# A graph kernel's edge sort: the block-number comparison of a row is written with two tables instead of one and a scalar

## The chip, the cores and the metric

The kernel runs on one core of a Trainium2 chip. The metric is the device time of one execution in microseconds (us), as the median of several runs. A core has a matmul engine (PE, with its weight loads shown apart as PEld), a vector engine (DVE), an activation engine (ACT), GpSimd (POOL) and a queue engine that issues transfers (SP). They run their own instruction streams and meet only at semaphores.

## The reference

A graph of 6,250 nodes with 64 features and 200,000 edges goes through four layers, each added to its input and normalised over the features. What matters here is that every layer gathers rows of the source nodes and sums them at the destination nodes:

```python
edge_index = jnp.stack([src, dst])
x = _layernorm(x + _L0_gnn_ref(x, edge_attr_8, edge_attr_16, edge_weight, ..., src, dst), axis=-1)
x = _layernorm(x + _L1_gnn_ref(x, edge_index, edge_weight), axis=-1)
x = _layernorm(x + _L2_gnn_ref(x, edge_index, L2_gnn_W1, L2_gnn_b1, L2_gnn_W2, L2_gnn_b2), axis=-1)
x = _layernorm(x + _L3_gnn_ref(x, edge_index, L3_gnn_W1, L3_gnn_b1, L3_gnn_W2, L3_gnn_b2), axis=-1)
```

Layer 0 also computes, for each edge, `silu(edge_feats @ W1 + b1) @ W2 + b2` for two sets of attributes. Those two small networks are evaluated while the edges are sorted.

## The kernel before

Nodes are split into 50 blocks of 125 by their number modulo 50. `prepare` works out each edge's block numbers and writes a row of sort keys (`key_rows`) and a row of destination block numbers (`block_rows`, bf16) to memory. `sort_edges`, the function that the change touches, then moves each edge into the bucket of its pair (destination block, source block): a memory row of 70 numbers goes to a slot that is the bucket's start plus the edge's rank in it. Later stages (`build_graph`, `smooth`, `polynomial`, `convolve`) work on the sorted rows. A barrier of all engines stands between the sort and `build_graph`.

The sort runs over 200 groups of 8 tiles of 125 edges (1,000 edges), with two sets of buffers `u` used in turn. For each group:

- SP loads `key_row`, `block_row` and `attrs`, once DVE has released the rows (`rows_read`) and PE has read the attributes (`hidden_ps`).
- DVE, in `group_hots`, copies the group's table (L345) and makes three one-hot tables by comparison: `hot_d` and `hot_s` (125 x 400, L352 and L353) from a table of block numbers and a column of each edge, and `hot_dt` (50 x 1000, L354), which has the block number in the partition and the edge along the row. The semaphore `hots` is raised by L354.
- PE waits for `hots`, and for each of the 8 tiles multiplies the running `count` with `hot_dt` (`ps_r`, L300), adds the tile's own counts (`ps_c`, L304), and lets ACT copy the new count (L272). Between them it does the two halves of the hidden layer (`ps_h`, L293) and the output layer (`ps_m`, L314), and after the second tile two small products for the group before (`ps_f`, L321 and L323), which need DVE's `spills` (L383, semaphore `flagged`).
- DVE, in `places`, which it runs for the group before the one whose one-hot tables it has just made, computes the rank of each edge (`same`, L373, eight times; `picked`, L379; `base`, L381), forms the output rows (L387 to L390), waits for `ps_f` (L392) and ends with the slot numbers `row_at` (L401).
- POOL issues 8 indirect transfers per group (L243), which read `row_at` and write the rows to their slots.

On DVE the order is written out by hand: one-hot tables of a group, then the places of the group before, with nothing in parallel. The column `lane_col` holds each partition's own number in float32.

Of the kernel before, what the change touches and what calls it, by code (L numbers as in the profile page):

```python
# [10 lines left out]
NB = 50  # L11
NL = N_NODES // NB
TE = 125
NT = N_EDGES // TE
G = 8
# [120 lines left out]
def sort_edges(nc, io, tbl, key_rows, block_rows, sorted_rows, zeros, zeroed, n_spilled):  # L136

    with ExitStack() as ctx:
# [13 lines left out]
        block_row = [sb(f"block_row{u}", [NB, G * TE], BF16) for u in two]  # L152
# [4 lines left out]
        hot_dt = [sb(f"hot_dt{u}", [NB, G * TE], BF16) for u in two]  # L157
# [19 lines left out]
        lane_col = sb("lane_col", [TE, 1], F32)  # L177
# [16 lines left out]
        with nc.Block() as blk:  # L194
# [139 lines left out]
            def _(dve):  # L334
# [5 lines left out]
                def group_hots(g, it, u, first):  # L340
                    g_is_0 = isinstance(g, int) and g == 0
                    dve.wait_ge(loaded[u], 64 * it + 64)
                    if not first:
                        dve.wait_ge(mixed, g - 1)
                    dve.tensor_copy(grp[u][:, :, 0:8], tbl[:, bass.ds(g * G, G), :]).then_inc(step, 1)  # L345
                    dve.wait_ge(step, 1 if g_is_0 else STEPS * g - (STEPS - 2))
                    dve.scalar_tensor_tensor(grp[u][:, :, 8], grp[u][:, :, 6], float(NB), grp[u][:, :, 7],
                                             ALU.mult, ALU.add)
                    dve.scalar_tensor_tensor(grp[u][:, :, 9], grp[u][:, :, 6], float(NB * CAP), grp[u][:, :, 7],
                                             ALU.mult, ALU.add)  # L350
                    iota3 = iota_blocks[:].unsqueeze(1).to_broadcast([TE, G, NB])
                    dve.tensor_tensor(hot_d[u][:], iota3, grp[u][:, :, 6:7].to_broadcast([TE, G, NB]), ALU.is_equal)  # L352
                    dve.tensor_tensor(hot_s[u][:], iota3, grp[u][:, :, 7:8].to_broadcast([TE, G, NB]), ALU.is_equal)  # L353
                    dve.tensor_scalar(hot_dt[u][:], block_row[u][:], lane_col[0:NB, 0:1], None,  # L354
                                      ALU.is_equal).then_inc(hots, 1)

                def link(ins, value):
# [6 lines left out]
                def places(g, it, u, done):  # L364
# [37 lines left out]
                    assert k[0] == STEPS - 1  # L402

                group_hots(0, 0, 0, True)
                group_hots(1, 0, 1, True)
                places(0, 0, 0, 1)
                with dve.Fori(1, NG // 2) as it:
                    group_hots(2 * it, it, 0, False)
                    places(2 * it - 1, it - 1, 1, 1)
                    group_hots(2 * it + 1, it, 1, False)  # L410
                    places(2 * it, it, 0, 1)
# [1550 lines left out]
```

## Time and profile before

| | us |
|---|---|
| median of 3 runs | 8770.59 |
| lowest and highest run | 8768.96, 8785.42 |
| profiled execution, its own time | 8773.64 |
| span of that execution | 8771.9 |
| PE busy over the span | 6998.2 |
| DVE busy over the span | 5907.1 |
| ACT busy over the span | 4550.5 |
| POOL busy over the span | 2836.6 |
| first and last transfer of the sorted rows starts at | 448.33, 2910.12 |

The busy times are those of the span of 8771.9 us; 1.7 us of the execution lie outside it. The last row tells where the sort lies in the span: about 28% of it. The span's 40 equal slices are 219 us each, so the sort fills slices 3 to 14.

### The profile page before, as it was taken

To read this page: it belongs to the slowest core of one execution; us is meant where nothing else is said; L and a number is where in the kernel's file an instruction comes from. 1 tells how busy PE (TensorE), PEld (TensorE's weight loads), DVE (VectorE), ACT (ScalarE), POOL (GpSimd) and SP (SyncE) were. 2 spreads that over 40 slices of the span, in tenths; PEclk is the share of its full clock that TensorE was granted. 3 is DMA by queue.
4 is the path that set the end of the run, shared out by engine and by line. 5 is a ranking of instruction groups with operands and counts; after the bars stand their busy time and mean duration, and the time that the engine had idled before them with its cause. 6 is when DMAs were issued, how large, how long until landed. Compare 5 with 4: busy or idle time off the path is not lost. (4 is left out here: it accounts for less than half of the span.)

```text
span 8771.9 us, 281023 instructions
## 1 busy us (share of the span) xinstructions
PE 6998.2 (80%) x98174; PEld 5919.3 (67%) x98174; DVE 5907.1 (67%) x15840; ACT 4550.5 (52%) x14713; POOL 2836.6 (32%) x2937
## 2 busy tenths in 40 slices
PE   0399999999999789889883886887876878876876
PEld 0155555555555788888873786776875878875766
DVE  1277766666777788888875886886785655555555
ACT  0222222222222688888873997997983444443443
POOL 0078888888888544444440000000000000000000
PEclk9999999999999999999996998998998989887978
DMA  9222222322222466666664887887874545542534
GB/s 385 82 58 60 60 59 60 60 60 60 59 59 60 151 205 208 204 204 208 202 191 149 286 288 245 286 285 246 290 252 139 178 157 166 172 157 95 173 127 135
DMA packets 781209, 1430.10 MB, mean 163 GB/s; under 512 B 294298, under 2 KB 361580, under 8 KB 776696
## 3 DMA queue, kind: packets, MB, share of 16 engines
q1 hardware_dynamic: 571720, 967.63, 35.6%
q10 hardware_dynamic: 116928, 381.29, 12.6%
q0 software_dynamic: 92048, 74.42, 4.3%
q8 instruction: 312, 5.11, 0.2%
q14 instruction: 201, 1.65, 0.1%
HBM read 987.87 MB, written 433.30 MB: 162 GB/s over the span
## 5 line engine op out<-in xcount | busy, mean ns | idle before, releaser
L243 POOL DMA_INDIRECT sorted_rows<-sort_rows,sort_row_at x1600 | 1975.6, 1235 | 519.1 <-issue 506.0
L1452 ACT ACTIVATE smooth_msg<-smooth_ps_l,smooth_w_rows 128x64 f32<-128x64 f32 x7500 | 1591.3, 404 | 224.2 <-PE smooth_ps_l L1516 210.2
L272 ACT ACTIVATE sort_count<-sort_ps_c 50x50 bf16<-50x50 f32 x1600 | 331.2, 207 | 1984.0 <-PE sort_ps_c L304 1983.9
L1210 PE MATMUL poly_ps<-parts,poly_cast 125*128 125x192 bf16 x12500 | 1089.5, 252 | 203.4 <-DVEq L1289 106.3
L1210 PEld LDWEIGHTS poly_ps<-parts,poly_cast 125*128 125x128 bf16 x12500 | 1073.6, 101 | 219.0 <-issue 135.4
L1176 ACT ACTIVATE poly_cast<-poly_mat 128x1280 bf16<-128x1280 uint8 x500 | 609.2, 1262 | 771.1 <-PE poly_ps L1210 550.5
L1516 PE MATMUL smooth_ps_l<-parts,smooth_src 125*128 125x64 bf16 x22500 | 800.3, 195 | 261.3 <-DMA smooth_src<-src_rows 151.6
L1516 PEld LDWEIGHTS smooth_ps_l<-parts,smooth_src 125*128 125x128 bf16 x22500 | 720.1, 99 | 302.4 <-ACT smooth_msg L1452 130.1
L314 PE MATMUL sort_ps_m<-sort_w,sort_hidden 128*125 128x64 f32 x3200 | 879.3, 430 | 0.0
L1530 PE MATMUL smooth_ps_s<-smooth_msg,smooth_hot 128*128 128x64 bf16 x7500 | 763.5, 194 | 133.3 <-DVE smooth_last_part L1664 106.3
L300 PEld LDWEIGHTS sort_ps_r<-sort_count,sort_hot_dt 50*125 50x125 bf16 x1600 | 283.2, 177 | 835.8 <-issue 583.3
L1661 DVE TENSOR_TENSOR smooth_rest<-smooth_msg 128x640 f32<-128x640 f32 x750 | 617.7, 824 | 305.9 <-ACT smooth_msg L1452 265.2
L293 PE MATMUL sort_ps_h<-sort_attrs,sort_w 24*128 24x500 f32 x800 | 811.6, 1115 | 2.5 <-DMA sort_attrs<-in_attr_t 2.5
L1530 PEld LDWEIGHTS smooth_ps_s<-smooth_msg,smooth_hot 128*128 128x128 bf16 x7500 | 684.7, 98 | 164.3 <-issue 116.2
L701 ACT ACTIVATE graph_hot_t<-graph_ps_t 128x1024 bf16<-128x1024 bf16 x625 | 641.8, 1027 | 289.4 <-PE graph_ps_t L744 267.6
L1530 PE MATMUL smooth_ps_s<-smooth_rest,smooth_hot 128*128 128x64 bf16 x7500 | 761.1, 194 | 3.1 <-issue 3.1
L1530 PE MATMUL smooth_ps_s<-smooth_last_part,smooth_hot 128*128 128x64 bf16 x7500 | 759.7, 193 | 4.1 <-issue 4.1
L314 PEld LDWEIGHTS sort_ps_m<-sort_w,sort_hidden 128*125 128x125 f32 x3200 | 732.1, 320 | 41.2
L777 PE MATMUL graph_ps_kv<-kv_parts,graph_hot_t 125*128 125x128 bf16 x7500 | 694.4, 221 | 0.0
L1530 PEld LDWEIGHTS smooth_ps_s<-smooth_last_part,smooth_hot 128*128 128x128 bf16 x7500 | 683.6, 99 | 4.2 <-issue 4.2
L1530 PEld LDWEIGHTS smooth_ps_s<-smooth_rest,smooth_hot 128*128 128x128 bf16 x7500 | 685.1, 98 | 1.1 <-issue 1.1
L671 POOL TENSOR_TENSOR graph_parts<-graph_parts 128x260 f32<-128x260 f32 x625 | 388.5, 622 | 912.5 <-DVE graph_hot L828 909.9
(313 smaller groups left out, 14892.5 us busy)
## 6 DMA issues: line engine op xcount, KB each, us to landing
smooth_src<-src_rows SPq DMA_DIRECT2D x750, 320.0 KB, 4.3
smooth_hot<-hot_rows SPq DMA_DIRECT2D x750, 320.0 KB, 4.7
poly_mat<-counts_t ACTq DMA_DIRECT2D x504, 400.0 KB, 3.6
sorted_rows<-zeros ACTq DMA_DIRECT2D x100, 875.0 KB, 13.4
graph_edges<-sorted_rows SPq DMA_DIRECT2D x125, 700.0 KB
conv_mat<-counts ACTq DMA_DIRECT2D x208, 400.0 KB, 3.6
hot_rows<-graph_hot SPq DMA_DIRECT2D x125, 640.0 KB, 3.6
src_rows<-graph_hot_t SPq DMA_DIRECT2D x125, 640.0 KB, 3.5
```

The costliest lines, as they stand in the source:

```text
L243: pool.indirect_dma_start(out=sorted_rows, out_offset=bass.IndirectOffsetOnAxis(row_at[u][:, j:j + 1], 0), in_=rows[u][:, j, :], in_offset ...
L293: nc.tensor.matmul(ps_h[h][:, 0:H * TE], w1[:], attrs[u][:, h * H * TE:(h + 1) * H * TE], start=True, stop=True).then_inc(hidden_ps, 1)
L314: last = nc.tensor.matmul(ps_m[u][0:TE, t * D:(t + 1) * D], hidden[u][:, t * TE:(t + 1) * TE], w2[:], start=True, stop=True, skip_group_ch ...
L671: pool.tensor_tensor(p[:, :, GROUP:2 * GROUP], p[:, :, 0:GROUP], high(p, 0), ALU.subtract)\
L701: act.activation(hot_t[x.b][:, :, :, x.s, :].rearrange("p e t v d -> p e t (v d)"), ps_t[x.g % 2][:].rearrange("p e t v d -> p e t (v d)") ...
L777: last = nc.tensor.matmul(ps_kv[u][:, 2 * t + v], s_t, kv_parts[:, s, i], start=i == 0, stop=i == 2, skip_group_check=True)
L1176: act.activation(cast[u][h][:, DVE_S:HR, :], mat[u][h][:, DVE_S:HR, :], ACT.Copy)\
L1210: last = nc.tensor.matmul(ps[u][:, 0:3 * D], cast[u][h][0:NL, s, :], parts[:, b].rearrange("p i d -> p (i d)"), start=b == 0, stop=b == NB ...
L1452: last = act.activation(at[:, s, :], ps_l[g % 2][h][:, i * D:(i + 1) * D], ACT.Copy, scale=w_rows[:, u, c * CHUNK + s:c * CHUNK + s + 1])
L1516: last = nc.tensor.matmul(ps_l[g % 2][h][:, i * D:(i + 1) * D], src[c][0:NL, b, :], parts[k % 2][:, c * CHUNK + b, j, :], start=j == 0, st ...
L1530: last = nc.tensor.matmul(ps_s[u][:, 0:D], hot[c][:, i // 2, :, i % 2], part[:, i, :], start=c == 0 and i == 0 and j == 0, stop=c == N_CHU ...
L1661: dve.tensor_tensor(rest[c][:], msg[c][:], high(msg[c]), ALU.subtract).then_inc(firsts, 1)
```

## The change

One instruction of `group_hots` is written in another form, with the same result. In the old form each element of `block_row` is compared with one number that its partition holds, given as a scalar operand. In the new form it is compared, element by element, with a second table operand, and that table is the same column read again for each of the 1,000 elements.

```diff
@@ group_hots @@
-                    dve.tensor_scalar(hot_dt[u][:], block_row[u][:], lane_col[0:NB, 0:1], None,
+                    dve.tensor_tensor(hot_dt[u][:], block_row[u][:], lane_col[0:NB, 0:1].to_broadcast([NB, G * TE]),
                                       ALU.is_equal).then_inc(hots, 1)
```

Every engine has the same number of instructions in the same order as before, with the same waits. `hot_dt` and `block_row` are bf16 and `lane_col` is float32 in both forms.

## Rows read from the trace of the kernel before

**Rows 1.** The page: PE's busy share and granted clock, tenths, in 40 slices.
```profile
PE   0399999999999789889883886887876878876876
...
PEclk9999999999999999999996998998998989887978
```
**Rows 2.** Busy us, 1600 to 2200: PE, PEld, DVE, ACT, POOL, then granted clock.
```profile
1600.00:2200.00 600.00, 570.99 (x1856) 356.06 (x1856) 409.03 (x1851) 138.86 (x490) 480.94 (x391) 1.00 0.28 59
```
**Rows 3.** PE in order of time: start, length; the same step in three groups.
```profile
430.17 0.30 PE L300 MATMUL sort_ps_r<-sort_count,sort_hot_dt 50*125 50x50 bf16 x1
...
442.48 0.30 PE L300 MATMUL sort_ps_r<-sort_count,sort_hot_dt 50*125 50x50 bf16 x1
...
2879.85 0.30 PE L300 MATMUL sort_ps_r<-sort_count,sort_hot_dt 50*125 50x50 bf16 x1
```
**Rows 4.** Who waited for whom, 400 to 2700 us: total, times, longest (us).
```profile
DVE sort_spill_ps L392 <- PE sort_ps_f L323: 465.0, 184, 2.9
...
PE sort_ps_r L300 <- ACT sort_count L272: 109.8, 371, 0.3
...
PEld sort_ps_r L300 <- DVE sort_hot_dt L354: 1.5, 1, 1.5
```
**Rows 5.** Instructions on the tile of L354: count, shortest/median/longest in ns.
```profile
L354 DVE TENSOR_SCALAR sort_hot_dt<-sort_block_row,sort_lane_col x200: 464/481/905, 429.6 to 2873.6; 50x1000 bf16<-50x1000 bf16 x100
```
**Rows 6.** DVE's groups by line, 300 to 2800 us: busy us, mean ns.
```profile
L389 DVE TENSOR_TENSOR sort_rows<-sort_biased,sort_grp 125x512 f32<-125x512 f32 x192 | 133.0, 692 | 6.5
...
L354 DVE TENSOR_SCALAR sort_hot_dt<-sort_block_row,sort_lane_col 50x1000 bf16<-50x1000 bf16 x194 | 115.1, 594 | 0.0
```
**Rows 7.** The page's costliest groups: busy us, mean ns, idle before.
```profile
L243 POOL DMA_INDIRECT sorted_rows<-sort_rows,sort_row_at x1600 | 1975.6, 1235 | 519.1 <-issue 506.0
...
L1661 DVE TENSOR_TENSOR smooth_rest<-smooth_msg 128x640 f32<-128x640 f32 x750 | 617.7, 824 | 305.9 <-ACT smooth_msg L1452 265.2
```
**Rows 8.** All engines in order of time, from 2923.85 us, after the sort.
```profile
2923.85 2.10 DVE L828 TENSOR_TENSOR graph_hot<-graph_iota,graph_lanes 128x512 bf16<-128x512 bf16 x6
```
**Rows 9.** One group in order of time, 1507 to 1518 us.
```profile
1507.71 0.47 DVE L354 TENSOR_SCALAR sort_hot_dt<-sort_block_row,sort_lane_col 50x1000 bf16<-50x1000 bf16 x1
...
1511.88 0.17 DVE L383 TENSOR_SCALAR sort_spills<-sort_rank 125x8 bf16<-125x8 f32 x1
...
1513.45 0.18 PEld L300 LDWEIGHTS sort_ps_r<-sort_count,sort_hot_dt 50*125 50x125 bf16 x1 [1.47 <-issue]
...
1516.20 0.27 PE L321 MATMUL sort_ps_f<-sort_spills,sort_before 125*125 125x8 bf16 x1
```
**Rows 10.** DVE in order of time, 2860 to 2925 us, with idle time before.
```profile
2870.71 0.17 DVE L392 COPY sort_spill_ps<-sort_ps_f 125x16 f32<-125x16 f32 x1 [1.64 <-PE sort_ps_f L323]
...
2884.36 0.17 DVE L401 TENSOR_TENSOR sort_row_at<-sort_spill_row,sort_slot_row 125x8 int32<-125x8 f32 x1
```
**Rows 11.** DVE in order of time, 424 to 450 us: the first group.
```profile
429.56 0.47 DVE L354 TENSOR_SCALAR sort_hot_dt<-sort_block_row,sort_lane_col 50x1000 bf16<-50x1000 bf16 x1
...
446.98 0.17 DVE L401 TENSOR_TENSOR sort_row_at<-sort_spill_row,sort_slot_row 125x8 int32<-125x8 f32 x1
```
**Rows 12.** POOL in order of time: sort's first transfer and three of its last.
```profile
448.33 1.78 POOL L243 DMA_INDIRECT sorted_rows<-sort_rows,sort_row_at  x1 [31.74 <-issue]
...
2898.17 1.19 POOL L243 DMA_INDIRECT sorted_rows<-sort_rows,sort_row_at  x1 [0.30 <-issue]
2899.67 1.19 POOL L243 DMA_INDIRECT sorted_rows<-sort_rows,sort_row_at  x1 [0.30 <-issue]
...
2911.61 1.19 POOL L248 DMA_INDIRECT sorted_rows<-zeros,sort_pad_at  x1 [0.30 <-issue]
```
**Rows 13.** All engines in order of time, 497 to 500 us.
```profile
497.79 1.55 POOL L243 DMA_INDIRECT sorted_rows<-sort_rows,sort_row_at  x1 [0.30 <-issue]
...
498.68 0.90 DVE L354 TENSOR_SCALAR sort_hot_dt<-sort_block_row,sort_lane_col 50x1000 bf16<-50x1000 bf16 x1
```
**Rows 14.** All 200 of line L352: shortest/median/longest in ns.
```profile
L352 DVE TENSOR_TENSOR sort_hot_d<-sort_iota_blocks,sort_grp x200: 562/569/571, 428.6 to 2872.7; 125x400 bf16<-125x400 f32 x100
```

## The prediction

> **What bounds the kernel now.** I read the page's slices first, for where the change lies: it touches only the sort, some 28% of the span, and there PE is at 9 tenths or more in every slice at full granted clock (0.9 and over in the row) [rows 1]. The other 72% runs the same instructions behind a barrier, so the question is what sets the sort's pace. The table of busy times by stretch gives it: in 600 us PE is busy for 570.99, POOL for 480.94, DVE for 409.03, at a granted clock of 1.00 [rows 2]. DVE, on which the changed instruction runs, is busy for 68% of the time.
>
> A share is no proof, so the order of time comes next. PE starts the same product of a group at 430.17 and, one group on, at 442.48: 12.31 us. The last group's is at 2879.85, which is 198 groups after 442.48, again 12.31 each [rows 3]. The rhythm doesn't move by a hundredth over 2,400 us. What PE waits for is ACT, 0.3 us at a time; it waited for DVE's line L354 once, for 1.5 us, in the first group [rows 4]. It is the other way round: DVE waits for PE's `ps_f`, 465.0 us in 184 waits, 2.53 us each [rows 4]. That is DVE's reserve in each group.
>
> The third engine is POOL, and it is closer to the edge than its share tells. Its last 9 transfers start from 2899.67 to 2911.61, so 8 of them take 11.94 us [rows 12]. From the first (448.33) to the first of the last group (2899.67) there are 199 groups of 12.32 us [rows 12]. So 0.38 us a group is not plain issuing. The page has the reason: the mean transfer took 1235 ns, where an undisturbed one takes 1190 [rows 7, 12], and 0.045 x 1600 is 72 us, which is 0.36 a group. POOL's instructions are being stretched, one of them to 1.55 us just where L354 itself took 0.90 [rows 13]. Without the stretching POOL would have 3% to spare beside PE's rhythm; with it, nothing.
>
> **The changed instruction.** L354 runs 200 times, 464 ns at the least, 481 in the median and 905 at the most [rows 5]; its mean is 594 [rows 6]. The trace has no comparison of this size with two tables. The nearest rows with a float32 table are `rows` with 512 elements, 692 ns [rows 6], and `smooth_rest` with 640, 824 ns [rows 7]: 132 ns for 128 elements, 1.03 ns each. From 640 on to 1,000 that gives 824 + 360 x 1.03 = 1195, so **1.20 us**. From below: a comparison of two bf16 tables of 512 took 2.10 / 6 = 0.35 us [rows 8]; scaled to 1,000 that is 0.68. From above: 692 scaled whole, 692 x 1000 / 512, is 1.35. I take 1.20, because the second table is float32, as in the rows that cost 1.03 ns an element, and not bf16 as in the cheap one. So the change adds 0.61 us of DVE work a group in the mean, 0.73 where L354 was undisturbed at 0.47: 200 x 0.61 = 122 us, and DVE goes from 68% to about 73%.
>
> **What covers those 122 us.** Three things wait for DVE behind L354.
> 1. PE waits for the one-hot tables. In the group at 1507 us L354 ends at 1508.18 and PE loads the first of its tiles at 1513.45 [rows 9]: 5.27 us of reserve, 4.54 afterwards.
> 2. PE's prefix products need `spills`, which ends at 1512.05; they start at 1516.20 [rows 9]: 4.15, afterwards 3.42.
> 3. DVE's own tail of the group needs `ps_f` and comes out in `row_at`, for which POOL waits. DVE stands idle for 2.53 us before it in the mean, and for 1.64 in a group where other instructions were held up [rows 4, 10]. After the change at least 1.64 - 0.73 = 0.91 is left, so `row_at` still comes at PE's time and not at DVE's. At the upper price of 1.35 it is 0.76.
>
> SP's loads are issued after `same`, up to 0.73 later, and DVE asks for them only in its next group. If all this cover were gone, each us above it would cost 200 us, since every group would pay. The term is **0**.
>
> **The head.** The first group has no cover: L354 runs from 429.56 to 430.03 [rows 11] and PE starts on its result at 430.17 [rows 3]. With 1.20 us it ends at 430.76 and PE starts at 430.90. Everything behind shifts by **+0.73 us**, once. The second group's table is needed only at 442.48.
>
> **The tail.** The sort ends with POOL's transfers, and here the change may give something back. `row_at` of the last group but one ends at 2884.53 [rows 10]; with the shift 2885.26. In the first group POOL started 1.18 us after `row_at` (447.15 to 448.33) [rows 11, 12]. An unstretched POOL would so begin that group at 2886.44 and the last one 11.94 later, at 2898.38; it does at 2899.67 [rows 12]. That is -1.3 at best, already with the head's shift in it; with POOL as late as now it is +0.7. The stretch depends on whether the new form disturbs POOL. L352 is such an instruction (a comparison with two tables in the same memory): 200 of them took 562 to 571 ns [rows 14], never held, while L354's time doubles when it meets POOL [rows 5, 13]. So I expect L354's part of POOL's stretch to vanish and some from the small copies to stay, and take **-1.0 us** for head and tail together.
>
> **The sum.** Against the profiled execution's own 8773.64 us: 0 from 200 groups, -1.0 from the ends: 8772.6. That execution lies 3.05 above the median of the runs shown (8770.59), so the forecast for the median is **8769.6 us**: no difference that can be measured. Within 0.2% (17.5 us) this kernel's measurement can't tell a change from none.
>
> **Rivals.**
> - *POOL is held by the new form.* It is longer, 1.20 us, and has two tables as inputs; POOL's transfers read `row_at` from the same memory. Were each of the 200 to hold POOL for its whole length, a group would take POOL 11.94 + 1.20 = 13.14 us, 0.83 above PE's 12.31; DVE waits for POOL's stores before it overwrites the rows, PE for DVE, and all fall into that step: 200 x 0.83 = 166 us, **8936 us**, slower. It decides from 0.37 us of holding a group on. For it: POOL has only that reserve and L354 does meet it [rows 13]. Against: L352's narrow spread [rows 14]. Chance 0.05.
> - The Trainium skill ("SBUF — State Buffer", Who interferes with whom) speaks against this change here: a DVE instruction with two SBUF inputs contends with a GpSimd instruction that reads SBUF. By that rule L352 and L353 should already be met and held at times, and the trace shows none of it; the same section infers that writing the descriptors, the other part of an indirect transfer, is left alone by such an instruction.
> - *DVE becomes the bound.* It needs L354 to grow by more than the idle 2.53 us, to over 3.1; at 3.5 us it would be 200 x 0.4 = 80, **8850 us**. No row has a cost above 1.35 ns an element that could give this. Chance 0.02.
> - *The stretch was the pace.* 11.94 + 0.36 is 12.30, suspiciously near 12.31. If POOL's stretch sets the rhythm, its removal gives up to 200 x 0.37 = 74 us, **8696 us**, faster. Against it: PE has the step of 12.31 between 430.17 and 442.48, before POOL's first transfer at 448.33 [rows 3, 12]. Chance 0.04.
> - *The edit does nothing to the instruction.* If the hardware reads the repeated column as cheaply as a bf16 table (0.68 us), the head costs 0.2 instead of 0.7 and the tail is the same: 8769 to 8770, no difference. Chance 0.05.
>
> **Chances and range.** My forecast has 0.83, and 0.01 is left for a median off by more than 17.5 us in a later stage, where the granted clock falls to 0.6 in a slice [rows 1]. Within 0.2%: 0.83 + 0.05 = 0.88. Faster: 0.04. Slower: 0.05 + 0.02 + 0.01 = 0.08. The terms alone give 8769.3 to 8771.3. What widens it is the measurement: three runs of one kernel lay between 8768.96 and 8785.42. I take 8763 to 8785, which leaves out the rivals with a measurable effect (0.11) and some 0.06 of scatter.
>
> **What the changed profile would show.** L354 as a table comparison of 1.15 to 1.25 us with a narrow spread; PE's step still 12.31 us; DVE's wait before L392 down by some 0.6 us a group, from 2.53 to about 1.9; PE's start on `ps_r` at 0.7 later in the first group; a mean transfer on POOL near 1200 ns in place of 1235; the last transfer within 1.5 us of 2911.61. The prediction is wrong if PE shows waits for `hot_dt` or `spills` beyond the first groups, or if the mean transfer grows past 1240 ns.

## The result, and the profile after the change

The changed kernel takes **8842.59 us** in the median (8835.41 to 8854.78), the kernel before 8770.72 in the same comparison: a ratio of 1.008, with a 95% interval of 1.0062 to 1.0097. That is 72 us slower. The prediction was 8769.6 us with a range up to 8785, so it was wrong, and on the side of the rival to which it gave 0.05.

The time is lost in the sort. POOL, in order of time, from the changed kernel; the columns are start, length, and idle time before:

```profile
2971.97 1.20 POOL L243 DMA_INDIRECT sorted_rows<-sort_rows,sort_row_at  x1 [0.30 <-issue]
...
2983.96 1.20 POOL L248 DMA_INDIRECT sorted_rows<-zeros,sort_pad_at  x1 [0.30 <-issue]
```

The last transfer starts at 2983.96 instead of 2911.61 [rows 12]: 72.35 us later. The span grew by 8840.1 - 8771.9 = 68.2, so the later stages add nothing to the loss. The same stretch of 600 us as in [rows 2], with the columns named there:

```profile
1600.00:2200.00 600.00, 556.03 (x1805) 346.88 (x1804) 441.77 (x1801) 133.62 (x473) 484.77 (x379) 1.00 0.28 58
```

PE does less in it (556.03 us for 570.99), DVE more, and POOL handles 379 instructions for 391 in slightly more busy time. The instructions themselves tell more. First all of the tile of L354 and all of POOL's transfers (shortest/median/longest in ns), then from the page the transfers' busy time and mean:

```profile
L354 DVE TENSOR_TENSOR sort_hot_dt<-sort_block_row,sort_lane_col x200: 1179/1183/1227, 428.7 to 2943.5; 50x1000 bf16<-50x1000 bf16 x100
```
```profile
L243 POOL DMA_INDIRECT sorted_rows<-sort_rows,sort_row_at x1600: 1185/1195/2240, 448.1 to 2982.5; - x178
```
```profile
L243 POOL DMA_INDIRECT sorted_rows<-sort_rows,sort_row_at x1600 | 2048.2, 1280 | 519.3 <-issue 517.8
```

L354 takes 1.18 us, as forecast (1.20), with the narrow spread forecast. But the mean transfer went from 1235 ns [rows 7] to 1280, where I expected about 1200, and the longest is 2.24 us. 1600 x 0.045 is 72 us: the whole loss. Who waited for whom, 400 to 2700 us of the changed kernel (total, times, longest in us):

```profile
DVE sort_biased L387 <- DMA sorted_rows<-sort_rows,sort_row_at: 393.5, 161, 4.8
...
PE sort_ps_f L321 <- DVE sort_spills L383: 39.2, 54, 1.3
DVE sort_spill_ps L392 <- PE sort_ps_f L323: 27.7, 14, 2.9
```

DVE's 465.0 us of waiting for PE [rows 4] has turned into 393.5 us of waiting for POOL's transfers to land, because it may not overwrite rows that are still being stored. PE in turn waits for DVE. PE's step shows it:

```profile
442.22 0.30 PE L300 MATMUL sort_ps_r<-sort_count,sort_hot_dt 50*125 50x50 bf16 x1
...
2945.31 0.30 PE L300 MATMUL sort_ps_r<-sort_count,sort_hot_dt 50*125 50x50 bf16 x1
```

(2945.31 - 442.22) / 198 is 12.64 us for the 12.31 of [rows 3]. POOL has become the bound of the sort.

**What holds a transfer.** Two places of the changed kernel in order of time. In the first, L354 runs when POOL's transfer starts:

```profile
799.93 1.18 DVE L354 TENSOR_TENSOR sort_hot_dt<-sort_block_row,sort_lane_col 50x1000 bf16<-50x1000 bf16 x1
799.95 2.24 POOL L243 DMA_INDIRECT sorted_rows<-sort_rows,sort_row_at  x1 [0.30 <-issue]
```
```profile
1513.47 0.57 DVE L352 TENSOR_TENSOR sort_hot_d<-sort_iota_blocks,sort_grp 125x400 bf16<-125x400 f32 x1
1513.55 1.56 POOL L243 DMA_INDIRECT sorted_rows<-sort_rows,sort_row_at  x1 [0.30 <-issue]
...
1513.96 0.57 DVE L353 TENSOR_TENSOR sort_hot_s<-sort_iota_blocks,sort_grp 125x400 bf16<-125x400 f32 x1
1514.44 1.18 DVE L354 TENSOR_TENSOR sort_hot_dt<-sort_block_row,sort_lane_col 50x1000 bf16<-50x1000 bf16 x1
...
1515.41 1.28 POOL L243 DMA_INDIRECT sorted_rows<-sort_rows,sort_row_at  x1 [0.30 <-issue]
```

L354 ends at 801.11, the transfer at 802.19: 1.08 later. L352 ends at 1514.04, the transfer that began under it at 1515.11: 1.07. The second L354 ends at 1515.62, its transfer at 1516.69: 1.07. An undisturbed transfer takes 1.19. So it seems to need something 0.12 us after its start that DVE holds until a two-table instruction ends, and 1.07 us from there on. The kernel before had this too. DVE's rows where I had blamed L354 [rows 13]:

```profile
497.71 0.57 DVE L352 TENSOR_TENSOR sort_hot_d<-sort_iota_blocks,sort_grp 125x400 bf16<-125x400 f32 x1
498.19 0.57 DVE L353 TENSOR_TENSOR sort_hot_s<-sort_iota_blocks,sort_grp 125x400 bf16<-125x400 f32 x1
```

L352 ends at 498.28, and the transfer of 1.55 us that started at 497.79 [rows 13] ends at 499.34: 1.06 later. L354, beginning at 498.68, came after the transfer had got through. I went over all 1,600 transfers of both traces in this way and added up what each took over 1.19, by the instruction whose end lies 1.07 us (within 0.04) ahead of the transfer's end. Before: `same` 28 us, L352 21, L389 17, L353 7. After: **L354 60 us in 121 transfers**, L389 33, L352 23, `same` 19, L353 8. Only 1 clearly stretched transfer in each trace fits none of these, the sort's first. The converse holds too: in the changed kernel 903 transfers had no instruction with two tables in SBUF (the memory that holds all tiles here but those named `ps_`) running 0.12 us after their start, and none of them took over 1.23 us.

The old L354 did have a part, though. Of `same`'s 28 us in the kernel before, 22 are 43 transfers that were due to get in while L354 ran, and got in only when the first `same` behind it had ended:

```profile
1618.03 0.47 DVE L354 TENSOR_SCALAR sort_hot_dt<-sort_block_row,sort_lane_col 50x1000 bf16<-50x1000 bf16 x1
1618.10 1.73 POOL L243 DMA_INDIRECT sorted_rows<-sort_rows,sort_row_at  x1 [0.30 <-issue]
...
1618.42 0.34 DVE L373 SCALAR_TENSOR_TENSOR sort_same<-sort_key_row,sort_grp,sort_before 125x125 bf16<-125x125 int16 x1
```

That `same` ends at 1618.76 and the transfer 1.07 us later, at 1619.83. So the old form, with a scalar, was not harmless to POOL either; in this trace it held fewer transfers, and for less time (0.54 us at the most, against 1.05 in the changed kernel).

### The profile page after: what moved, and what is told of

Same layout as the page of the kernel before. It is cut to its first block and busy times, and to the rows that moved or that the text cites. A ratio compares the mean times of both kernels' runs of the same rounds, so it can differ in the third digit from the quotient of the medians.

```text
span 8840.1 us, 280998 instructions
## 1 busy us (share of the span) xinstructions
PE 6997.5 (79%) x98149; PEld 5917.6 (67%) x98174; DVE 6041.1 (68%) x15840; ACT 4540.5 (51%) x14713; POOL 2907.7 (33%) x2937
## 5 line engine op out<-in xcount | busy, mean ns | idle before, releaser
L243 POOL DMA_INDIRECT sorted_rows<-sort_rows,sort_row_at x1600 | 2048.2, 1280 | 519.3 <-issue 517.8
```

Of the source, the lines that this page charges most:

```text
L243: pool.indirect_dma_start(out=sorted_rows, out_offset=bass.IndirectOffsetOnAxis(row_at[u][:, j:j + 1], 0), in_=rows[u][:, j, :], in_offset ...
```

## The experiments

Each kernel was timed beside runs of the kernel before on the same chip. Three theories stand against one another. A: a DVE instruction with two tables in SBUF holds POOL's transfer. B: DVE's longer work is enough by itself. C: the total time that DVE spends in two-table instructions counts, in whatever pieces. The tiles named `ps_` lie in PSUM, the memory that PE writes its products to. The edits are cut to the lines that matter.

### One of the two tables in PSUM

```diff
+                dve.tensor_copy(ps_f[0:NB, 200:201], lane_col[0:NB, 0:1]).then_inc(laned, 1)
+                dve.wait_ge(laned, 1)
...
-                    dve.tensor_tensor(hot_dt[u][:], block_row[u][:], lane_col[0:NB, 0:1].to_broadcast([NB, G * TE]),
+                    dve.tensor_tensor(hot_dt[u][:], block_row[u][:], ps_f[0:NB, 200:201].to_broadcast([NB, G * TE]),
```

> The changed comparison, with the column of lane numbers read from PSUM, so that only one of its two tables lies in SBUF. Theory A (a transfer that POOL begins while DVE runs an instruction with two tables in SBUF is held until it ends): L354 still takes about 1.2 us, no transfer is held to 2.2 us by it, the mean transfer falls from 1280 to 1235 ns or less, PE's step is 12.31 us, and the time is 8765 to 8775 us. Theory B (DVE's longer instruction alone makes DVE, then PE, late): nothing changes, 8842 us.

Measured: 8780.10 us beside 8775.22, ratio 1.0006 (0.9996 to 1.0015). L354's successor, line L356, takes the same time, and the transfers are back at their old mean. Groups by line of this kernel (busy us, mean ns), then the stretch of 600 us:

```profile
L356 DVE TENSOR_TENSOR sort_hot_dt<-sort_block_row,sort_ps_f 50x1000 bf16<-50x1000 bf16 x200 | 236.1, 1181 | 0.0
```
```profile
L243 POOL DMA_INDIRECT sorted_rows<-sort_rows,sort_row_at x1600 | 1974.2, 1234 | 519.5 <-issue 516.2 <-DVE sort_row_at L403 3.0 <-DVE sort_pad_at L417 0.3
```
```profile
1600.00:2200.00 600.00, 571.00 (x1857) 356.11 (x1857) 444.28 (x1855) 138.52 (x490) 480.93 (x391) 1.00 0.29 60
```

DVE is as busy as in the changed kernel (444.28 us for 441.77) and PE is back at 571.00. The instruction itself holds nothing any more: 192 transfers had L356 running 0.12 us after their start, and none of these took over 1.24 us. The median lies 5 us above the expected range, which was set around 8770; the kernel before stands at 8775.22 in this comparison. The whole loss went with the place of one operand. B falls.

### One table, as slow

```diff
-                    dve.tensor_tensor(hot_dt[u][:], block_row[u][:], lane_col[0:NB, 0:1].to_broadcast([NB, G * TE]),
-                                      ALU.is_equal).then_inc(hots, 1)
+                    dve.tensor_scalar(hot_dt[u][:], block_row[u][:], lane_col[0:NB, 0:1], None,
+                                      ALU.is_equal, ALU.add, accum_out=row_hits[:]).then_inc(hots, 1)
```

> The old form with its scalar, and with the sum of its results written out as well, which should take it out of the fast rate: a long instruction (about 1.2 us, and a short read of the sum) with one table. Theory A: POOL isn't held by it, the mean transfer is 1235 ns or less, 8765 to 8775 us. Theory B: DVE has as much to do as after the change, so 8842 us or a little more.

Measured: 8778.47 us beside 8775.22, ratio 1.0004 (0.9994 to 1.0014). From the groups by line:

```profile
L355 DVE TENSOR_SCALAR_CACHE_REDUCE sort_hot_dt<-sort_block_row,sort_lane_col 50x1000 bf16<-50x1000 bf16 x200 | 247.8, 1239 | 0.0
```

It takes 1239 ns, more than the changed L354, and costs nothing measurable; the median is 3 us above the expected range, and above the kernel before by as much. 195 transfers had it running 0.12 us after their start, and none took over 1.23 us. Length alone doesn't hold a transfer; at this length it takes the second table in SBUF.

### Seven transfers for eight

```diff
-                        for j in range(G):
+                        for j in range(G - 1):
                             pool.indirect_dma_start(
...
-                    dve.wait_ge(stored[u], 16 * G * it)
+                    dve.wait_ge(stored[u], 16 * (G - 1) * it)
```

The rows that would stay unwritten are filled with zeros ahead of the sort, so both kernels leave out every eighth tile of edges, and their output isn't the graph's. The changed kernel so cut:

> The changed kernel with 7 of a group's 8 transfers (every eighth tile of edges is left out of the sorted rows, and the rows it would leave unwritten are filled with zeros). Theory A: POOL needs 7 x 1.49 + 0.7 = 11.2 us a group, under PE's 12.31, so the two-table form costs nothing: 8765 to 8775 us, as the kernel before with 7 transfers. Theory B: DVE's work is the same, so some 70 us above that kernel.

The kernel before so cut:

> The kernel before with 7 of a group's 8 transfers (the same work left out). Theory A and B: PE's step stays 12.31 us, 8765 to 8775 us. Were POOL's stretching the pace of the kernel before, it would be 50 us or more below 8770.

Measured: 8775.21 us (ratio 0.9999, 0.9990 to 1.0009) and 8772.62 us (0.9999, 0.9989 to 1.0008), beside 8775.22. With time to spare on POOL the two-table form costs nothing, so the loss does go through POOL. The second run settles the rival in which POOL's stretch was the pace of the kernel before: POOL had one transfer in eight less to issue and the time stayed. From that kernel's groups by line:

```profile
L245 POOL DMA_INDIRECT sorted_rows<-sort_rows,sort_row_at x1400 | 1794.8, 1282 | 694.5 <-issue 535.2 <-DVE sort_row_at L403 159.0 <-DVE sort_pad_at L417 0.3
```

Its mean transfer is 1282 ns, as long as in the changed kernel, and harmless, since POOL waits 159.0 us for DVE anyway. A mean transfer alone doesn't tell a cost.

### The two-table form beside the old one

```diff
+                    dve.tensor_tensor(spare[:], block_row[u][:], lane_col[0:NB, 0:1].to_broadcast([NB, G * TE]),
+                                      ALU.is_equal)
                     dve.tensor_scalar(hot_dt[u][:], block_row[u][:], lane_col[0:NB, 0:1], None,
```

> The kernel before with its one-table form, and ahead of it the two-table form as an additional instruction into a tile that nobody reads. Theory A: the additional instruction is held against POOL as in the changed kernel, mean transfer about 1280 ns, 8830 to 8880 us. If the slowdown came from the removal of the one-table form, and not from the presence of the long two-table one: 8770 us.

Measured: 8821.89 us beside 8779.24, ratio 1.0039 (1.0025 to 1.0054), mean transfer 1256 ns. The direction is A's, and the longest transfer is 2236 ns, beside 2240 in the changed kernel; but the size, 43 us, is under my range, and so is the mean transfer. Counted as above, the additional instruction held 133 transfers for 50 us, while `same` and L389's successor held theirs for 28 us less than before. All holding together grew by 35 us, which lies inside the interval of the loss (22 to 47 us). How often a transfer starts under an instruction seems to depend on where the two engines' patterns lie to one another, and I could not compute that ahead.

### A bf16 table

`lane_row` is the column written out once, ahead of the sort, as a bf16 tile of 50 x 1000.

```diff
-                    dve.tensor_tensor(hot_dt[u][:], block_row[u][:], lane_col[0:NB, 0:1].to_broadcast([NB, G * TE]),
-                                      ALU.is_equal).then_inc(hots, 1)
+                    dve.tensor_tensor(hot_dt[u][:], block_row[u][:], lane_row[:], ALU.is_equal).then_inc(hots, 1)
```

> The two-table form with the second table written out in bf16 for all 1,000 elements, which should take 0.6 to 0.7 us in place of 1.18. Theory A: a transfer that it meets is held for 0.7 us at the most, about a third of the changed kernel's holding, mean transfer 1235 to 1255 ns, 8770 to 8800 us. Theory C: 8780 to 8810 us, in proportion to the time in two-table instructions.

Measured: 8780.51 us beside 8779.24, ratio 1.0002 (0.9992 to 1.0011). The instruction takes 664 ns, the lower price of the prediction nearly to the number (0.68), and the mean transfer is 1234 ns. It does hold transfers, 98 of them for 40 us, but `same`, L352's and L389's successors held less than before, and all holding together is 71 us, for 72 in the kernel before. So this two-table form costs nothing here, because the sum still fits what POOL can spare. The time lies in the ranges of A and of C alike; beside a kernel before of 8779.24 the 1 us of difference is less than C's proportion (664 of 1183 ns, some 40 us) would give.

### L352 and L353 with one table in PSUM, L354 with two in SBUF

```diff
+                dve.tensor_copy(ps_f[0:TE, 256:256 + NB], iota_blocks[:]).then_inc(laned, 1)
...
-                    iota3 = iota_blocks[:].unsqueeze(1).to_broadcast([TE, G, NB])
+                    iota3 = ps_f[0:TE, 256:256 + NB].unsqueeze(1).to_broadcast([TE, G, NB])
```

> The changed kernel, with the table of block numbers of L352 and L353 read from PSUM, so that these two have one table in SBUF and L354 keeps two. Theory A: the stretches that now end 1.07 us after L352 and L353 (about 30 us over the sort) go, those of L354 stay, so the loss shrinks but doesn't vanish: 8790 to 8825 us. If only L354 can hold POOL, nothing changes: 8842 us.

Measured: 8779.09 us beside 8779.24, ratio 1.0000 (0.9990 to 1.0009). More than A promised: the loss is gone altogether, though L354 is the changed one. Counted as above, the two with a table in PSUM stretch nothing to speak of (198 transfers had one of them running 0.12 us after their start, and one of these was long, 1.37 us, the sort's first), while L354 still stretches 40 transfers by 18 us. So L354 isn't the culprit alone. Together the instructions hold POOL for more than it can spare, and taking away others does as well.

### In pieces

Eight pieces of 125 elements:

```diff
+                    for j in range(G):
+                        last = dve.tensor_tensor(hot_dt[u][:, j * TE:(j + 1) * TE], block_row[u][:, j * TE:(j + 1) * TE],
+                                                 lane_col[0:NB, 0:1].to_broadcast([NB, TE]), ALU.is_equal)
+                    last.then_inc(hots, 1)
```

> The changed comparison in eight pieces of 125 elements, each with two tables. DVE spends more time on it in total (8 x 0.2 to 0.3 = 1.6 to 2.4 us against 1.18). Theory A in its sharper form (a transfer that starts inside one two-table instruction ends 1.07 us after that instruction, so what counts is the length of a single instruction): no hold from these pieces over 0.3 us, POOL stays within 12.31 us a group, 8768 to 8790 us. Theory C (what counts is the total time in which DVE works with two tables): 8842 us or more.

Measured: 8891.51 us beside 8779.24, ratio 1.0122 (1.0105 to 1.0139), worse than the change itself. My sharper form of A is wrong. In order of time:

```profile
500.46 2.03 POOL L243 DMA_INDIRECT sorted_rows<-sort_rows,sort_row_at  x1 [0.30 <-issue]
501.09 0.33 DVE L375 SCALAR_TENSOR_TENSOR sort_same<-sort_key_row,sort_grp,sort_before 125x125 bf16<-125x125 int16 x1
```

The transfer ends at 502.49, 1.07 us after the end of the first `same` (501.42); it got in at none of the boundaries between the pieces that ran while it waited. The same happened wherever a transfer was due under the sixth or the eighth piece: all 147 of them were held until a first `same` had ended, by up to 0.86 us. After the first three pieces the way was open: 48 transfers ended 1.07 us after one of these, and cost 5 us in all. So the pieces don't act as one instruction of 1.67 us (their whole length), but a row of them can hold for longer than any one does, and the `same` behind them belongs to the row. To part DVE's own additional time from this, the same eight pieces with the column in PSUM, and then two pieces of 500 in SBUF:

```diff
-                                                 lane_col[0:NB, 0:1].to_broadcast([NB, TE]), ALU.is_equal)
+                                                 ps_f[0:NB, 200:201].to_broadcast([NB, TE]), ALU.is_equal)
```

> The eight pieces again, with the column of lane numbers read from PSUM. DVE's time for them is the same as in the eight pieces before (1.67 us a group), but only one table lies in SBUF. Theory A: POOL's mean transfer goes back from 1308 to 1235 ns and the time to 8765 to 8790 us. Theory B (DVE's additional time, by itself, is what made the eight pieces slow; PE waited for their end there, 24.8 us in 34 waits): 8850 to 8895 us.

Measured: 8781.53 us beside 8771.32, ratio 1.0009 (0.9999 to 1.0018), pieces of 271 ns for 275, mean transfer 1234 ns. 198 transfers were due under the pieces, and none of them took over 1.21 us. All but some 10 us of the 112, and that not clear of nothing, is holding.

```diff
+                    for h in two:
+                        last = dve.tensor_tensor(hot_dt[u][:, h * H * TE:(h + 1) * H * TE],
+                                                 block_row[u][:, h * H * TE:(h + 1) * H * TE],
+                                                 lane_col[0:NB, 0:1].to_broadcast([NB, H * TE]), ALU.is_equal)
```

> The changed comparison in two pieces of 500 elements (about 0.66 us each), both tables in SBUF. If a transfer can get in between two long instructions, as it does between L352 and L353 in the changed kernel, no hold is longer than 0.66 us: mean transfer 1235 to 1260 ns, 8770 to 8810 us. If the boundary between two pieces is closed, as it is between the eight short ones, holds of up to 1.1 us remain, and the time is 8835 to 8860 us.

Measured: 8795.03 us beside 8771.32, ratio 1.0030 (1.0018 to 1.0043). The mean transfer is 1238 ns. The longest, 1779, is the sort's first and tells nothing (1777 in the kernel before); the next is 1721, a hold of 0.53 us, and no transfer due under the first piece was held past that piece's end. So the boundary between two pieces of 665 ns is open, and the loss of 24 us is a third of the change's. C fits the eight pieces but not these two, which have more time in two-table instructions (2 x 665 = 1330 ns) than the change (1183) and lose less.

## Why the prediction was wrong

- **The price of L354** was right: 1.183 us for 1.20 forecast. So was its narrow spread.
- **DVE's cover** was right: with the column in PSUM the same 1.18 us cost nothing measurable. PE's step stayed, and DVE still waited 427.5 us for `ps_f` there, 2.3 us in each of 184 waits, where I had said 1.9.
- **The head** was under 1 us, as forecast: PE waited 0.56 us for L354 in the first group. Its first product doesn't start later by that in the span, as I had written, but at 429.90 for 430.17, because what runs ahead of it differs by more between executions.
- **The tail is the step that failed**, in the sentence that L352, "never held", shows that a two-table instruction doesn't disturb POOL, "so I expect L354's part of POOL's stretch to vanish". POOL's stretch grew by 72 us instead, from 72 to 144, so that the 200 groups, put at 0, cost some 72, and the ends gave nothing back. L352's narrow spread tells that *it* isn't held. Whether it holds another stands in the other engine's rows: [rows 14] could not bear what I rested on them, and the sentence among the rivals that the trace shows none of the contention was wrong too. The row that could was in [rows 13], a transfer of 1.55 us, and I put it down to L354, which is the longest thing near it, without comparing ends. Its end lies 1.06 us after L352's.
- **What the rows before held besides.** The whole trace of before had more: all 57 transfers that were due under L352, and all 57 under L389, were stretched; under L379 and L387, as long (0.57 and 0.69 us) but with one of their tables in PSUM, 74 and 93 were due, and not one took over 1.21 us ("due" is here 0.12 us after the start, and 0.04 us clear of either end of the instruction). In these DVE kept its time and POOL paid. With the old L354 it went both ways: 57 of its 200 took 0.90 us, each ending 0.24 us after a transfer that was under way when it began (as in [rows 13]), and 43 transfers were held under it.
- **The rival that came true** was priced at 8936 us, with a hold of L354's whole length in each of the 200 groups. It holds 121 of the 1,600 transfers, for 0.5 us in the mean: 60 us. Its point of decision, 0.37 us of holding a group, was right: the kernel before stood on it, with 8 x (1.235 - 1.19) = 0.36, and the changed kernel is at 8 x (1.280 - 1.19) = 0.72, so all that was added went into the time.
- The Trainium skill ("SBUF — State Buffer", Who interferes with whom) had said it: a DVE instruction with two SBUF inputs contends with a GpSimd instruction that reads SBUF. The run with one input in PSUM agrees (1234 ns for 1280). The section also infers that such an instruction leaves the issue of transfers from GpSimd alone, because writing descriptors needs the write interface; the indirect transfers here were held by up to 1.05 us (2.24 for 1.19), so for them the measurement decides against it.
- **Why the trace of before hid it.** POOL's 1235 ns looked like a stretch that could go away. It is the mean that any content gives as long as POOL runs without a pause at PE's pace: 12.31 / 8 - 0.305 of gap = 1.234 us, and 1234 or 1235 ns is what the kernel before, the two kernels with the column in PSUM, the slow one-table form and the bf16 table show (with L352 and L353's table in PSUM it is 1230, and POOL waits for DVE 16 us in all). My reading of it: POOL catches up until its starts fall under DVE's two-table instructions, and is held there just as long as it has time for. A full row like that says that an engine has no visible pause left, not how much is in reserve.
- **Left open**: why a transfer gets in between two instructions of 0.57 us or more, and after the first pieces of 0.28, but not after the later ones, nor between the old L354 and the first `same`; and what exactly the transfer needs at 0.12 us from its start. Reading its row of slots, `row_at`, is the obvious candidate, but no run moved it.

No version here beats the kernel before. PE's step is 12.31 us a group in it, and a POOL with less to do gave nothing.

## What to carry to other kernels

When DVE and GpSimd's indirect transfers overlap, count a DVE instruction with two tables in SBUF as time in which such a transfer seems to get no further than its first 0.12 us. Here GpSimd was within a few per cent of the pace, and a longer two-table instruction, or a row of short ones back to back, went straight into the time; one operand in PSUM, a shorter type, or a long form with one table and a scalar took the cost out again. Add up the holding of all instructions, since the sum decides and not the one that was changed. Read interference on the victim's rows, by comparing its ends with the other engine's ends; an engine whose own durations never vary may be the one that always wins. Splitting an instruction to let another engine in can make it worse.

## What the runs showed of the hardware

- An indirect transfer on POOL that takes 1.19 us undisturbed ends 1.07 us (within 0.04) after the end of the DVE instruction with two tables in SBUF that ran 0.12 us after its start; the longest was 2.24 us. With one of the two tables in PSUM none was held (192 transfers under L356, none over 1.24 us).
- A comparison of a table with a scalar in its fast form (0.47 us) held 43 transfers up to the end of the first `same`, by 0.54 us at the most, and took 0.90 us itself, 57 times of 200, ending 0.24 us after a transfer that was under way when it began.
- A table comparison of 1,000 elements on 50 partitions took 1183 ns with the second table in float32 (repeated column, in SBUF), 1181 with it in PSUM, 664 with both in bf16, 1239 as a one-table form that also sums.
- In a row of eight two-table comparisons of 0.275 us, back to back, transfers got in after the first three, but all 147 that were due under the sixth or eighth were held past the row's end, by up to 0.86 us; between two of 0.665 us they got in.
